# The quantised layer and the long convolution as one turn each, with transforms on even and odd tokens

## The reference

```python
def _L1_ffn_ref(input, weight, bias):
    FP8_MAX = 448.0
    def quant_fp8(x):
        amax = jnp.max(jnp.abs(x)).astype(jnp.float32)
        scale = jnp.minimum(FP8_MAX / jnp.maximum(amax, 1e-12), FP8_MAX)
        x_fp8 = jnp.clip(x * scale, -FP8_MAX, FP8_MAX).astype(jnp.float8_e4m3fn)
        return (x_fp8, 1.0 / scale)
    ...
    acc = jnp.matmul(x_fp8.astype(jnp.float32), w_fp8.astype(jnp.float32).T)
    out2d = (acc * (x_scale * w_scale) + bias).astype(jnp.bfloat16)

def _L2_attn_ref(x, proj_w, proj_b, filter_time):
    p = (jnp.einsum('bld,de->ble', x, proj_w) + proj_b).reshape(B, L, order + 1, D)
    v = p[:, :, 0, :]
    for stage in range(order):                      # order = 2
        vf = jnp.fft.rfft(v, n=fft_size, axis=1)
        ff = jnp.fft.rfft(filter_time[stage], n=fft_size, axis=1)
        conv = jnp.fft.irfft(vf * ff, n=fft_size, axis=1)[:, :L, :]
        v = conv * p[:, :, stage + 1, :]
    return v
...
x = _layernorm(x + _L1_ffn_ref(x, ...), axis=-1)
x = _layernorm(x + _L2_attn_ref(x, ...), axis=-1)
```

## Time and profile before

| what | value |
|---|---|
| median of three runs (2854.62 to 2860.02) | 2859.42 us |
| the profiled execution | 2862.32 us |
| its span, first to last instruction | 2860.6 us |
| mean granted TensorE clock, as a share of 2.4 GHz | 0.90 |
| TensorE busy (MATMUL) | 2333.3 us, 82% |
| VectorE busy | 1433.5 us, 50% |
| ScalarE busy | 1025.7 us, 36% |
| GpSimd busy | 672.5 us, 24% |

### The profile page before, as it was taken

How to read it: one execution, slowest core, us unless ns; L and a number is a source line. 1 busy time by engine, 2 the same in 40 slices (tenths; PEclk the granted TensorE clock), 3 DMA queues, 4 the chain that set the end, 5 groups by cost and what they waited for, 6 DMA issues and landing times. The chain is left out here.

```text
span 2860.6 us, 38992 instructions
## 1 busy us (share of the span) xinstructions
PE 2333.3 (82%) x12834; PEld 1622.3 (57%) x12834; DVE 1433.5 (50%) x4235; ACT 1025.7 (36%) x2587; POOL 672.5 (24%) x609
## 2 busy tenths in 40 slices
PE   7983599878789438878667879879799899899898
PEld 5762477655467324447246656546356577466576
DVE  3554122447668554345412266645577543577454
ACT  3432111155446200006212226534366543466432
POOL 1113311200034102210443310065343200434111
PEclk9996799979789669988688989989899999999899
DMA  9041211290000100002157721130000000000000
GB/s 236 2 191 48 74 46 35 70 132 1 1 7 1 39 17 0 0 8 115 47 160 208 199 74 27 30 139 1 30 1 2 1 1 0 1 1 1 19 23 19
DMA packets 121167, 143.58 MB, mean 50 GB/s; under 512 B 47507, under 2 KB 101013, under 8 KB 119184
## 3 DMA queue, kind: packets, MB, share of 16 engines
q1 hardware_dynamic: 112240, 120.16, 15.7%
q0 software_dynamic: 8736, 20.99, 2.0%
HBM read 96.18 MB, written 47.90 MB: 50 GB/s over the span
## 5 line engine op out<-in xcount | busy, mean ns | idle before, releaser
L249 PE MATMUL bank<-work,weights 128*128 128x256 f32 (+4 forms) x2048 | 491.4, 397 | 65.0 <-DMA work<-in_weights 29.4
L249 PE MATMUL bank<-weights,work 128*128 128x256 f32 (+4 forms) x1680 | 450.8, 409 | 26.5 <-ACT work L272 16.9
L249 PEld LDWEIGHTS bank<-work,weights 128*128 128x128 f32 (+1 forms) x2048 | 345.7, 195 | 182.0 <-issue 50.7
L249 PEld LDWEIGHTS bank<-weights,work 128*128 128x128 f32 (+1 forms) x1680 | 314.5, 199 | 130.3 <-issue 59.0
L633 POOL TENSOR_TENSOR work<-work,minus_half 128x2 f32<-128x2 f32 x80 | 57.7, 722 | 801.2 <-DVE work L626 801.2
L249 PE MATMUL bank<-weights,x_feat 128*128 128x512 f32 (+2 forms) x384 | 166.2, 557 | 24.2 <-PEq L211 13.2
L249 PE MATMUL bank<-x_feat,weights 128*128 128x256 f32 (+3 forms) x400 | 119.3, 473 | 35.7 <-PEq L211 31.0
L249 PE MATMUL bank<-work 128*128 128x120 f32 (+4 forms) x358 | 82.2, 373 | 78.9 <-DVE work L2268 47.3
L3958 ACT ACTIVATE work<-work 128x128 f32<-128x128 f32 (+1 forms) x256 | 137.5, 545 | 1.7 <-DVE work L4030 1.6
L1523 DVE TENSOR_TENSOR work<-bank,work 128x384 f32<-128x384 f32 (+1 forms) x64 | 31.4, 491 | 190.0 <-ACT work L1441 190.0
L249 PEld LDWEIGHTS bank<-x_feat,weights 128*128 128x128 f32 (+1 forms) x400 | 79.6, 217 | 64.9 <-issue 51.5
(11 more groups left out here) (462 smaller groups left out, 4750.2 us busy)
## 6 DMA issues: line engine op xcount, KB each, us to landing
weights<-in_weights SPq DMA_DIRECT2D x62, 256.0 KB
weights<-in_weights SPq DMA_DIRECT2D x1, 12296.0 KB, 35.5
weights<-in_weights SPq DMA_DIRECT2D x1, 9360.0 KB, 25.1
weights<-in_weights SPq DMA_DIRECT2D x1, 8488.0 KB, 23.9
work<-rows_in SPq DMA_DIRECT2D x62, 129.0 KB
rows_in<-ident SPq DMA_DIRECT2D x2, 3968.0 KB, 40.1
weights<-rows_back SPq DMA_DIRECT2D x8, 768.0 KB, 5.3
work<-rows_in SPq DMA_DIRECT2D x8, 645.0 KB, 4.2
```

The costliest lines, as they stand in the source:

```text
L249: ins = nc.tensor.matmul(out, lhsT, rhs, start=(i == 0), stop=(i == len(pairs) - 1))
```

## The change

**Side attention.** VectorE finds the peak of each batch of `x_tok` (`peak`) one step behind its normalise, and the peak of the next sublayer's weights at step 3, behind a wait for them. They go to the free end of the weights' second place (`quant_buffers`).

**Quantised layer.** One turn. The maximum over the partitions is taken by a turn on TensorE, a reduction and a turn back. Then steps of one batch: ScalarE scales (`scale_x`), VectorE clips and makes the power (`magnitude`, three operations of 512 columns), GpSimd adds and subtracts it (`rounded`), TensorE multiplies, VectorE adds bias and residual, and the shared tail follows. The residual is added in `x_tok` in place.

**Long convolution.** One turn, steps of one batch. With an odd frequency f and its mirror the cosine keeps its value on even tokens and changes its sign on odd ones, the sine the other way round. So the forward transform of a batch is taken at 128 frequencies, of even tokens and of odd tokens apart (`forward`: 4 products of 256 columns on half as many tokens each); the sum and the difference of the halves (`add_sides`) are the values at both. The first stage's transform back uses the same (`fold` on GpSimd, `backward_even_odd`: 4 products), and gives even and odd tokens apart, as the next forward wants them; the second stage's (`backward`: 8 products) gives the tokens in order. ScalarE copies the odd half to SBUF (`store_odd`), since an instruction reads only one of its operands from PSUM here. The complex product is two VectorE products of 1024 columns out of SBUF (`direct`, `crossed`) and one GpSimd addition of 1024 (`combine`). SyncE loads the tables' and filters' even and odd rows with eight loads at the head.

```diff
@@ side_attention, VectorE
+            def peak(b):
+                v.wait_ge(S.x_normed, b + 1)
+                nc.vector.tensor_reduce(q.peak[:, b:b + 1], K.x_tok[:, 2 * b:2 * b + 2, :].rearrange("p i d -> p (i d)"),
+                                        AX.X, ALU.max, apply_absolute_value=True)
...
+                if t == 3:
+                    weights_are_in(v, K, 5)
+                    nc.vector.tensor_reduce(q.peaks[:, 1:2], next_w.rearrange("p k d -> p (k d)"), AX.X, ALU.max,
+                                            apply_absolute_value=True)
@@ quantised_linear
+            def rounded(b):
+                p.wait_ge(S.k_rounded, b + 1)
+                nc.gpsimd.tensor_tensor(scaled[:, b % 2, :, :], scaled[:, b % 2, :, :], power[:, b % 2, :, :], ALU.add
+                                        ).then_inc(S.pool_step, 1)
...
+                nc.gpsimd.tensor_tensor(x16[:, b % 2, :, :], scaled[:, b % 2, :, :], power[:, b % 2, :, :], ALU.subtract
+                                        ).then_inc(S.xn_stored, 1)
...
+            a.wait_ge(S.inverse_done, 1)
+            for t in range(STEPS):
+                if (b := at_step(t, 1, B)) is not None:
+                    scale_x(b)
+                if (b := at_step(t - 2, 1, B)) is not None:
+                    batch_store(nc.scalar.copy, a, K, b, 2 + b % 2)
...
-    with nc.Fori(0, GROUPS) as g:
-        with turn(nc, K) as block:
...
+            for t in range(STEPS):
+                if (b := at_step(t, 1, B)) is not None:
+                    magnitude(b)
+                if t == 0:
+                    round_to_e4m3(nc, then, q.w16, W["w"], q.scale[:, 1:2], w_scaled, w_power).then_inc(S.root_done, 1)
+                if (b := at_step(t - 1, 1, B)) is not None:
+                    residual(b)
+                if (b := at_step(t - 2, 1, B)) is not None:
+                    batch_normalise(nc, v, K, tail, b)
@@ long_convolution, GpSimd
+                nc.gpsimd.tensor_tensor(spec[:, s, :, :, :], direct[:, q % 2, :, :, :], crossed[:, q % 2, :, :, :], ALU.add
+                                        ).then_inc(S.side_added, 1)
...
+                for which, op in ((0, ALU.add), (1, ALU.subtract)):
+                    ins = nc.gpsimd.tensor_tensor(folded[:, which, :, :], spec[:, 0, 0, :, :], spec[:, 0, 1, :, :], op)
@@ long_convolution, TensorE
+                    tokens = slice(b * L + i, (b + 1) * L, 2) if e < ORDER else slice(b * L + i * P, b * L + (i + 1) * P)
...
+            for t in range(STEPS):
+                if (b := at_step(t, 1, B)) is not None:
+                    forward(b, 0)
+                if (b := at_step(t + 1, 1, B)) is not None and b:
+                    project(b, 0)
+                    project(b, 1)
+                if (b := at_step(t - 1, 1, B)) is not None:
+                    backward(b)
+                if (b := at_step(t + 1, 1, B)) is not None and b:
+                    project(b, 2)
+                if (b := at_step(t, 1, B)) is not None:
+                    backward_even_odd(b)
+                if (b := at_step(t, 1, B)) is not None:
+                    forward(b, 1)
+                if (b := at_step(t - 2, 1, B)) is not None:
+                    turn_x(b)
@@ long_convolution, VectorE
+                for n, to, by in ((0, direct, filt), (1, crossed, filt_x)):
+                    ins = nc.vector.tensor_tensor(to[:, q % 2, :, :, :], x[:, :, n:n + 1, :].broadcast_to([P, 2, 2, D]),
+                                                  by[:, s, :, :, :], ALU.mult)
...
-    run_late(nc, K, t, body, bank=6)
```

More of the change, by code:

```diff
@@ L2051, in _, with quant_buffers @@
                         batch_normalise(nc, v, K, tail, 2 * g + i)
+def quant_buffers(K):
+    at = HIGH + words(5)
+    q = Names()
+    q.w16 = K.weights[:, at:at + KT * D // 2].bitcast(BF16).rearrange("p (k d) -> p k d", k=KT)
+    small = K.weights[:, at + KT * D // 2:at + KT * D // 2 + 32]
+    q.peak, q.peaks, q.most, q.scale, q.back = small[:, 0:B], small[:, 8:10], small[:, 10:11], small[:, 12:14], small[:, 14:16]
+    q.out_scale = small[:, 16:17]
+    return q
 def side_attention(nc, K):
@@ new lines, in _ @@
+            nc.vector.tensor_scalar(q.scale, q.scale, 448.0, 448.0, ALU.mult, ALU.min).then_inc(S.inverse_done, 1)
+            v.wait_ge(S.inverse_done, 1)
+            then(nc.vector.reciprocal(q.back, q.scale))
+            then(nc.vector.tensor_tensor(q.out_scale, q.back[:, 0:1], q.back[:, 1:2], ALU.mult))
+            for t in range(STEPS):
+                if (b := at_step(t, 1, B)) is not None:
[6 more added lines that the diff above has]
+                    batch_normalise(nc, v, K, tail, b)
@@ new lines, in filters, with forward @@
+            def filters(s):
+                for odd in range(2):
+                    for n in range(2):
+                        ins = mm(nc, K.bank[3 + 2 * s + odd][:, n * D:(n + 1) * D],
+                                 [(table[:, odd, n, :], taps[:, s, odd, :])])
+                ins.then_inc(S.aux_done, 1)
+            def forward(b, s):
+                q = 2 * b + s
+                if s:
+                    pe.wait_ge(S.gate_done, b + 1)
+                else:
+                    pe.wait_ge(S.q_stored, 3 * b + 1)
+                if q:
+                    pe.wait_ge(S.hid_stored, q)
+                else:
+                    pe.wait_ge(S.table_done, 1)
+                for odd in range(2):
+                    for n in range(2):
+                        ins = mm(nc, K.bank[HALVES[odd]][:, n * D:(n + 1) * D],
+                                 [(table[:, odd, n, :], gates[:, b % 2, 0, odd * D:(odd + 1) * D])])
+                ins.then_inc(S.scores_done, 1)
@@ L2379, in _ @@
+            weights_are_in(v, K, 6)
+            for e in range(ORDER + 1):
+                store_gates(0, e)
             for s in range(ORDER):
                 v.wait_ge(S.aux_done, s + 1)
[L2381 to L2466 removed]
```

399 lines of the change are left out of this document (257 added, 142 removed).

## The result

| what | before | after |
|---|---|---|
| median of four runs | 2858.53 us | 2787.09 us (2784.16 to 2790.38) |
| ratio, 95% interval | | 0.9752 (0.9736 to 0.9769) |
| the profiled execution, its span | 2862.32, 2860.6 us | 2786.11, 2784.4 us |
| quantised layer, first operation to last store | 83.1 us | 64.0 us |
| border behind it | 3.1 us | 1.2 us |

The changed kernel is 71.4 us faster. Forecast were 46 us, 2813.5.

A forecast was written before the change was run, and what follows sets the result against it. Bounds taken: TensorE in side attention, waits around VectorE in the quantised layer, a mostly TensorE chain in the convolution. Sum 0.5 + 67.5 + 1.5 + 200 = 269.5 for 315.5 us, 46 less: 2859.4 to 2813.5, range 2784 to 2846.

The forecast's parts named there:

- the main case: Whole kernel: the summed forecast of 2813.5 us, own range 2798 to 2830, given 55%.
- the first rival: Products and GpSimd's additions overlap, no exclusion: convolution ring 2.0 us a batch shorter, quantised ring 0.5; 2788 us, 12%.
- Peaks in side attention: Side attention: peak reductions added to VectorE would be hidden behind TensorE; 0.5 us taken, 6 us if uncovered.
- The layer's ring: Quantised layer: each batch one ring from ScalarE's scaling through VectorE, GpSimd and TensorE to ScalarE's store, 7.9 us.
- TensorE in the convolution: Long convolution: 32 products a batch instead of 44, 14.2 us for 19.5, and TensorE not the bound afterwards.
- The ring of a batch: Long convolution: VectorE's and GpSimd's operations, transforms and copy in one chain, 20.0 us a batch.
- Start and end: Long convolution: 10.9 us before the eight batches and 14.1 us after them.
- The clock: Long convolution: TensorE idling some 3 us drops its clock in five of eight batches, 3.0 us each, 15 us.
- Strides: Long convolution: even and odd tokens read as stationary operands two floats apart cost zero, since loads lie under products.
- The longer ring: GpSimd and VectorE handovers go the wrong way: 2.5 us a batch in the convolution, 1 in the quantised layer; 2842 us, 16%.
- The clock stayed up: Answers a rival: TensorE at clock 0.50 through the convolution, 30.6 us a batch, 2884 us, slower than before; 5%.
- The saved arithmetic: Answers a rival: the arithmetic saved was hidden and the turns cheap, so no change, 2859 us; 3%.

The follow-up runs named there:

- the scaling ahead: Changed kernel with ScalarE scaling batch b+1 of the quantised layer before storing batch b-2 instead of behind it: 2769.16 us, ratio to before 0.97.
- The late projection: Changed kernel with the next batch's third projection behind the second forward transform, and its gate bias behind the gate: 2802.05 us, one execution.
- the added GpSimd addition: Changed kernel with one more 512-column GpSimd addition per convolution batch, begun with the second stage's products: 2791.93 us; begun at the gate's end instead: 2781.45 us.

## Why the prediction was right, and where its sizes were off

The signs, the places and the order of the gains held: the layer's ring through ScalarE and the convolution's ring through VectorE and GpSimd were named before the result and shown by experiments. The sizes were off, and all one way: in the layer, the border and the convolution the gain was 65.4 us where 46.5 were forecast, and 15 of the 19 missing lie in the convolution. The time lies outside the range of the main case, which by its own bounds (-15 and -8, +9 and +3) should have been 2790 to 2826 and not 2798 to 2830, and outside that one too. The stated range held it because it took in the first rival's 2788, whose mechanism is refuted: that part is luck.

- *Peaks in side attention*, 0.5 us: 0, by the two rows at equal clock above. The layer starts 1.2 us earlier than before, inside the spread of 7.
- *Start of the layer*, 3.0: 3.3 (966.75 to 970.05).
- *The layer's ring*, 7.9 a batch: 7.6, its terms each within 0.2. The start and drain took 18 us for 20. The total, 67.5 (its terms add to 67.4), was 64.0. The 7.9 named a ring through ScalarE; the scaling ahead showed it.
- *Borders*, 1.5: 1.2.
- *TensorE in the convolution*, 14.2 a batch and no longer the bound: 74.7 us in five batches, 14.9 with the turns of 0.6. Right.
- *GpSimd's 1024 columns*, estimated 2.31 between 1.79 and 2.50: 2.36.
- *The ring of a batch*, 20.0 (its terms add to 19.9): 19.2. Two terms were not in it, the blocked normalise of 0.60 and the residual of 0.56 between the folds. I had VectorE slip in between GpSimd's instructions; in the trace GpSimd starts its fold 0.08 us behind the combine and VectorE waits, 2.82 and 1.03 us for 0.73 and 0.69. In their place stand 0.3 more from the transform back to the gate, which stands behind a gate's bias, and 0.1 of handovers. Over eight batches 6 us.
- *Start and end*, 10.9 and 14.1: 11.5 (1031.97 to the second subtract's end at 1043.46) and, at a lower clock, 16.6.
- *The clock*, 15 us by five falls of eight. This is the term that was off most. Its first step, "TensorE now idles some 3 us before the backward products and 1.5 before the next forward", was worked out as what is left of the ring. In the trace the idle pieces are 1.4, 1.0 and 1.8, since the second stage's transform back and the third projection lie right before; the granted clock is 1.00 in the five middle batches. Only the first batch (21.1 us), the last (20.3) and the end were slow, 5.6 us where 15 stood. The late projection made the 3.1 us real, and then five of the eight transforms back met a fall, at 2.3 to 2.5 us a batch in the middle of the stage: the price of 3.0 and the frequency nearly held, only the idle time didn't exist.
- *Strides*, 0: eight MATMULs out of odd and even columns took 2.00 us, eight out of contiguous ones 1.99 (1115.32 and 1099.12 above). Right.
- *The rivals.* No exclusion gave nearly the time, 2788, but not the mechanism: the added GpSimd addition cost 1.1 us a batch. The longer ring didn't come; GpSimd won the handovers before the fold, which is the better way round. The clock stayed up. The saved arithmetic was not hidden: made twice, it cost 36.5 us.
- *Behind the convolution* the two traces differ by 10 us that no term had; of the 71.4 us between the medians some 5 aren't in the stages touched. They fit the spread of unchanged stages, but no run shows that they are only that.

## What to carry to other kernels

Write the ring out instruction by instruction, and then write TensorE's own order beside it before pricing the clock: the idle pieces are what its queue leaves, not what ring minus work leaves. Here pieces of 1.0 to 1.8 us cost nothing in the middle of the stage, and a single one of 3.1 to 3.5 a batch cost 2.3 to 2.5 us where the clock fell, which it did not always do. Arithmetic on an engine that is no bound is still worth its full time where it stands in the ring: 36 us here. Where VectorE and GpSimd meet on SBUF, one waits for the other's whole instruction; moving small operations away doesn't free that time. A different order of two independent batches gave 27 us in the convolution, where moving the normalise then gave 5 and dropping the fold 2. And look at stages with unchanged code first: their length can differ with the granted clock of the execution.

## What the runs showed that was not expected

- An operation of 128x2 on VectorE took 1.92 us beside a 1024-column addition of GpSimd: the wait goes by the partner's rest, not by the own size (0.16 us alone). It lay wholly in the instruction's busy time, so VectorE's 91% was no measure of work.
- In the changed layer exclusion ran both ways within a microsecond: residual 1.20 for 0.69, subtraction 1.59 beside an addition of 1.26.
- Behind equal idle pieces of 3.1 us the granted clock once fell and once stayed, in neighbouring batches of one execution with the same instructions; in the last batch of the changed kernel it fell behind shorter ones.
- Stretches of identical code vary more than expected: the five sublayers behind the convolution (the changed ones are the fifth to seventh of twelve; 4 to 6 counts from 0) have the same code in all thirteen kernels and took 1560 to 1577 us. Side attention with the peaks took 164.1, 167.8 to 168.1 or 171.2 us, at a granted clock of 0.97, 0.94 or 0.92.
